# Window-attention block on one core: the gated product re-sorted by DMA, the projection in four quadrants, attention stages and channel units regrouped

## What is computed

```python
x_n = group_norm(x, 32 groups)                        # mean and variance of 2 channels over the image
qkv = einsum('bchw,oc->bohw', x_n, w_qkv) + b_qkv     # 1x1, 64 -> 192 channels
qkv = depthwise_conv3x3(qkv, w_dw) + b_dw             # padding 1
# windows of 8x8 pixels, 4 heads of 16 channels; x runs over the 64 pixels of a window
attn = softmax(einsum('nhcx,nhdx->nhcd', q, k) * temperature)
out  = einsum('nhcd,nhdx->nhcx', attn, v)
gate = gelu(einsum('nhcx,yx->nhcy', v, w_mlp) + b_mlp)
out  = out * gate
y    = x + einsum('bchw,oc->bohw', back_to_image(out), w_proj) + b_proj
```

## Time and profile before

| | |
|---|---|
| median of 3 runs | 679.36 us (678.96 to 680.39) |
| profiled execution, its own time | 681.82 us |
| its span, first to last instruction | 680.0 us |
| TensorE busy | 625.8 us (92%) |
| VectorE busy | 511.6 us (75%) |
| ScalarE busy | 482.8 us (71%) |
| mean granted TensorE clock | 0.973 |
| 16 DMA engines, share of the transfers of the SP queue | 31.0% |

### The profile page before, as it was taken

How to read it: one execution, slowest core, us unless ns; L and a number is a source line. 1 busy time by engine, 2 the same in 40 slices (tenths; PEclk the granted TensorE clock), 3 DMA queues, 4 the chain that set the end, 5 groups by cost and what they waited for, 6 DMA issues and landing times.

```text
span 680.0 us, 32438 instructions
## 1 busy us (share of the span) xinstructions
PE 625.8 (92%) x15044; PEld 549.1 (81%) x15044; DVE 511.6 (75%) x790; ACT 482.8 (71%) x631; POOL 0.3 (0%) x5
## 2 busy tenths in 40 slices
PE   3788799999999999999999999999999999999954
PEld 2687698888989898888989898888989798888843
DVE  4872688887888888786878676786868676876684
ACT  3652678787877778786877778786877778786722
POOL 0000000000000000000000000000000000000000
PEclk9997899999999999999999999999999999999975
DMA  9872115335171714132050504132150504112022
GB/s 363 263 217 72 33 50 166 110 86 208 33 232 49 234 59 149 66 102 93 8 191 5 195 4 142 60 94 106 29 173 4 198 3 152 44 50 80 4 82 44
DMA packets 29240, 72.28 MB, mean 106 GB/s; under 512 B 9801, under 2 KB 16329, under 8 KB 24233
## 3 DMA queue, kind: packets, MB, share of 16 engines
q1 hardware_dynamic: 28674, 68.57, 31.0%
q10 hardware_dynamic: 432, 1.65, 0.7%
HBM read 53.44 MB, written 16.78 MB: 103 GB/s over the span
## 4 chain that ended last, share of the span: by engine, by line
PE 87%; ACT 5%; DVE 3%; issue 2%; DMA 1%; ACTq 0%; DVEq 0%
PE unit_ps L709 28%; PE unit_ps L674 26%; PE rest_ps L796 10%; PE rest_ps L787 6%; PE rest_ps L763 6%; PE rest_ps L747 6%; PE rest_ps L773 4%; ACT z L326 2%; DMA patches<-in_hot 1%; ACT dw L326 1%; PE rest_ps L643 1%; PE rest_ps L674 1%; PE unit_ps L636 0%; DVE scores L511 0%; DVE scores L536 0%
## 5 line engine op out<-in xcount | busy, mean ns | idle before, releaser
L326 ACT ACTIVATE z<-unit_ps 100x768 f32<-100x768 f32 x244 | 184.9, 808 | 60.1 <-PE unit_ps L674 60.1
L674 PE MATMUL unit_ps<-consts,patches 64*100 64x192 f32 x1984 | 195.0, 336 | 8.6 <-ACT z L326 6.6
L709 PE MATMUL unit_ps<-z,dw 103*64 103x64 f32 (+2 forms) x6144 | 194.3, 224 | 3.0 <-issue 1.7
L709 PEld LDWEIGHTS unit_ps<-z,dw 103*64 103x64 f32 (+2 forms) x6144 | 185.5, 139 | 10.7 <-issue 8.6
L674 PEld LDWEIGHTS unit_ps<-consts,patches 64*100 64x100 f32 x1984 | 153.6, 164 | 25.8 <-ACT z L326 11.2
L326 ACT ACTIVATE qkv<-unit_ps 128x1024 f32<-128x1024 f32 x78 | 79.1, 1014 | 31.5 <-PE unit_ps L709 31.4
L511 DVE TENSOR_TENSOR scores<-rest_ps,consts 128x512 f32<-128x512 f32 x64 | 44.1, 689 | 51.6 <-PE rest_ps L747 51.6
L503 DVE TENSOR_TENSOR gate<-rest_ps,gate 128x512 f32<-128x512 f32 x64 | 44.1, 689 | 47.5 <-PE rest_ps L787 44.6
L796 PE MATMUL rest_ps<-gate,consts 128*128 128x256 f32 x256 | 75.1, 417 | 1.1 <-DVE gate L503 1.0
L347 ACT ACTIVATE v_t<-rest_ps 128x512 f32<-128x512 f32 x64 | 38.2, 597 | 40.5 <-PE rest_ps L773 38.9
L341 ACT ACTIVATE scores<-scores 128x512 f32<-128x512 f32 x64 | 40.4, 631 | 33.2 <-DVE scores L518 31.6
(11 more groups left out here) (55 smaller groups left out, 530.5 us busy)
## 6 DMA issues: line engine op xcount, KB each, us to landing
staged<-in_x SPq DMA_DIRECT2D x17, 1024.0 KB, 4.9
out_y<-staged SPq DMA_DIRECT2D x15, 1024.0 KB, 5.4
T<-in_x SPq DMA_DIRECT2D x12, 1152.0 KB, 6.7
seen<-in_x SPq DMA_DIRECT2D x32, 256.0 KB, 2.9
qkv<-in_x SPq DMA_DIRECT2D x6, 1024.0 KB, 13.9
T<-in_x SPq DMA_DIRECT2D x3, 1088.0 KB, 6.7
staged<-in_x SPq DMA_DIRECT2D x2, 512.0 KB, 22.9
out_y<-staged SPq DMA_DIRECT2D x4, 256.0 KB, 3.0
```

The lines of the kernel that those rows point to most:

```text
L326: return nc.scalar.activation(to, of, ACT.Copy)
L674: last = nc.tensor.matmul(to[0:NPATCH, t, b * QKV:(b + 1) * QKV], patches[image, b, g], w1[image], start=True, stop=True)
L709: last = nc.tensor.matmul(to[h * HW:(h + 1) * HW, m // 8, m % 8 * NW:(m % 8 + 1) * NW], dw[0:used, c, :], z[0:used, c, :], start=True, sto ...
```

## The change

1. **Projection.** Before, the gated product lay as VectorE wrote it (each 64-partition half holding a mixture of head halves), and two products with 128x128 stationary operands, mostly zeros, sorted and projected it. Now SP copies the gated product of a step with eight SBUF-to-SBUF transfers of 32x256 elements into `by_row` (`to_rows`), and four products with 64x64 stationary operands, one for each quadrant of the array, project it. It runs two steps later instead of one (`project(i - 2)` in step i), and the last step keeps the old form (`project_last`). `gate` has four buffers instead of three.
2. **Turning v.** In a0 and a1 `turn_v` makes eight products of 64 rows of v with a 64x64 identity instead of four transposes. a2 and a3 keep the transposes.
3. **Gates.** The gate products of step i+2 stand in steps a0 and a1, one each, and two in a3; one of those in a3 goes into a unit buffer. The first two stand before step 0, among the first depthwise units, together with their Gelus.
4. **Order.** Within a step TensorE does score, project, gates, turn_v, then all units of the step in one stretch, then apply_probs.

The core of the diff:

```diff
 def gates_in(i):
-    return (0, 1) if i == 0 else (i + 1, i + 2) if i % 2 and i + 2 < STEPS else ()
+    n, a = i // BATCHES + 1, i % BATCHES
+    if a < 2:
+        return (i + 2,)
+    return (i + 1, i + 2) if a == 3 and n < CHUNKS else ()
+
+def in_unit(j):
+    return j > 1 and j % BATCHES == 1
...
+            def to_rows(j):
+                sp.wait_ge(mixed_ready, j + 1)
+                if j > 1:
+                    sp.wait_ge(proj_done, j - 1)
+                for b in range(2):
+                    for h in range(2):
+                        for t in range(2):
+                            here, there = 2 * (h ^ b) + t, 2 * b + h
+                            sp.dma_start(by_row[there * BLOCK:(there + 1) * BLOCK, j % 2, t],
+                                         gate[here * BLOCK:(here + 1) * BLOCK, j % GATES, b].rearrange(
+                                             "p g y -> p (g y)")).then_inc(by_row_in[j % 2], 16)
...
+            for i in range(STEPS):
+                n, a = i // BATCHES, i % BATCHES
+                if i:
+                    to_rows(i - 1)
...
                 if a < 2:
-                    if more:
-                        evacuate_mix(act, copy, n, 8 * a)
-                        evacuate_mix(act, copy, n, 8 * a + 1)
-                    exponent(i)
-                    v_up(i)
-                    if more:
-                        for g in range(8 * a + 2, 8 * a + 6):
+                    if i == 0 or not more:
+                        v_up(i)
...
                     exponent(i)
                     if more:
+                        if i:
+                            for g in range(3):
+                                evacuate_mix(act, copy, n, 8 * a + g)
+                            v_up(i)
+                        for g in range(3 if i else 2, 6):
+                            evacuate_mix(act, copy, n, 8 * a + g)
...
                 n, a = i // BATCHES, i % BATCHES
                 dve.wait_ge(proj_done, i + 1)
+                if i + 2 < STEPS:
+                    dve.wait_ge(v_t_ready, i + 3)
...
             def turn_v(i):
...
+                    if i % BATCHES < 2:
+                        for h in range(2):
+                            rows = slice(h * HW, (h + 1) * HW)
+                            last = nc.tensor.matmul(turn_ps[:, h, g * HW:(g + 1) * HW], v[rows], ident[rows, rows],
+                                                    start=True, stop=True)
...
             def project(i):
 
+                pe.wait_ge(by_row_in[i % 2], 128 * (i // 2 + 1))
+                if i < STEPS - BATCHES:
+                    pe.wait_ge(mixed_ready, i + 2)
+                if i:
+                    pe.wait_ge(out_ready, i)
+                for t in range(2):
+                    for b in range(2):
+                        rows = slice(b * HW, (b + 1) * HW)
+                        last = nc.tensor.matmul(projected(i)[t * C:(t + 1) * C, b, :], proj_row[rows],
+                                                by_row[rows, i % 2, t].rearrange("p (g r c) -> p r g c", r=WS, c=WS),
+                                                start=True, stop=True)
...
-                if i % BATCHES == 0:
-                    qkv_of(i // BATCHES)
                 if i == 0:
-                    fill(units_now[:cut[0]])
-                score(i)
...
+                score(i)
...
+                if i > 1:
+                    project(i - 2)
+                for j in now:
+                    gates(j, i)
                 if i:
+                    turn_v(i)
+                fill(units_now[4:] if i == 0 else units_now)
+                if i == STEPS - 1:
                     project(i - 1)
-                turn_v(i)
-                fill(units_now[cut[0]:cut[1]])
-                if now:
-                    gates(now[1], i)
-                fill(units_now[cut[1]:cut[2]])
                 apply_probs(i)
-                fill(units_now[cut[2]:])
-            project(STEPS - 1)
+            project_last(STEPS - 1)
```

More of the change, by code:

```diff
@@ L66, in units @@
     for i in range(STEPS):
-        order += fillers(i)
+        order += [("gate", j) for j in gates_in(i) if in_unit(j)] + fillers(i)
     return {name: at for at, name in enumerate(order)}
@@ L365, in _ @@
             deviation(0)
-            exp_table(0)
             for g in range(0, COLS, 2):
                 evacuate_first(act, copy, g)
-            for v in range(0, 6, 2):
-                evacuate_dw(act, copy, 0, v)
+            evacuate_dw(act, copy, 0, 0)
+            evacuate_dw(act, copy, 0, 2)
+            gelu(0)
+            gelu(1)
+            exp_table(0)
+            evacuate_dw(act, copy, 0, 4)
             tables = 1
@@ L582, in _ @@
             normalise(1, 1)
-            for v in range(1, 6, 2):
-                evacuate_dw(dve, copy, 0, v)
+            evacuate_dw(dve, copy, 0, 1)
+            gate_up(0)
+            gate_up(1)
+            evacuate_dw(dve, copy, 0, 3)
+            evacuate_dw(dve, copy, 0, 5)
             for i in range(STEPS):
@@ L739, in score @@
                     pe.wait_ge(masked, i)
[L740 removed]
+                pe.wait_ge(gate_biased, max([2] + [beside_scores(j) for m in range(i) for j in gates_in(m)]))
                 for g in range(BATCH):
```

161 lines of the change are left out of this document (98 added, 63 removed).

## The result

The changed kernel takes **769.94 us** (median of four runs, 756.73 to 774.94) against 679.2 us: ratio **1.121** (95% interval 1.108 to 1.134). The ratio leaves out two of the four runs, which ran at a lower granted clock; the two in it took 767.0 and 756.7 us. It is slower, as forecast, but by twice as much as the 722 us of the forecast, and outside 700 to 742.

A forecast was written before the change was run, and what follows sets the result against it. TensorE, 92% busy, bounds the kernel before. +2.9 us a chunk gives +40.6 over fourteen; +2.4 statistics, -1 first chunk, +0.7 tail make +42.7 on 681.8: 724.5, less 2.5, 722 us; range 700 to 738, chance 0.76, or to 742.

The forecast's parts named there:

- the step that sets the sign: 1x1 units in a0 and a1: two buffers need 1.80 us for two units, against 1.30 us of TensorE work.
- The regrouping's saving: 1x1 units in one stretch: a pair needs 1.30 us instead of 1.53, saving some 1.5 us a chunk on TensorE.
- a0 and a1: First two steps of a chunk: 10.57 us each against 9.08 and 9.91, together +2.15 us.
- I keep 0.54: Turning v in a0 and a1: eight products take 0.54 us, with 0.85 as upper bound.
- The -0.10 forecast: Third step of a chunk, a2: 8.29 us, a change of -0.10 us.
- a3: Last step of a chunk: late first depthwise unit delays ScalarE's run, so next score comes at 11.5 against 10.67, +0.83 us.
- The regular part together: All four steps of a steady chunk: 40.94 us against 38.05, +2.9 us.
- The SP transfers stay off the path: Row transfers: eight issue in 2.5 us and land in 2.9, against at least 8.6 us until the projection needs them.
- Rival 4, the clock: Granted clock falls: one spell costs up to 6.9 us, three or more make it 740 us and up; chance 0.06.
- the chunks with statistics: Four chunks gathering the second pair's statistics: one more VectorE instruction ending a2 delays a3's product, +2.4 us in all.
- Head and tail: First chunk: -1 us, from a vanished stall and one pair of table loads; last four steps: +0.7 us.
- +0.5 a step at most: Last four steps, without units: v_up now before the exponent costs at most 0.5 us a step.

The follow-up runs named there:

- experiment 3: Changed kernel with v turned by transposes everywhere and units spread between the attention stages again, copies in old order: 688.85 us, ratio 1.017.
- Experiment 2: Changed kernel with v turned by four transposes in a0 and a1 too, instead of eight products: 752.23 us, ratio 1.110.
- experiment 9: Changed kernel with ScalarE copying only half of each 1x1 unit: 732.99 us, ratio 1.078.
- Experiment 10: Changed kernel with one depthwise unit of a3 directly behind the score again: 754.65 us, ratio 1.111.
- experiment 4: Kernel before, with eight idle row copies a step and the large store and load moved to a2 and a3: 703.0 us, ratio 1.037.
- 7: Changed kernel with transposes everywhere, units spread again, and large transfers early, in a0 and a1: 680.32 us, ratio 1.001.
- experiment 8: Changed kernel with the old projection, no row transfers, and large transfers early, in a0 and a1: 771.81 us, ratio 1.136.
- experiments 4 to 6: Besides experiment 4, kernel before with late large transfers and no copies, 688.23 us (1.014); with idle copies and large transfers at old places, 683.95 us (1.007).
- experiments 1: Changed kernel with the projection as before, two steps late, without row transfers: 771.99 us, ratio 1.139.

## Why the forecast had the sign and missed the size

**What bounds it, and the step that sets the sign: right.** The forecast read 1.80 us for two units through two buffers against 1.30 us of work, hidden by the attention stages between pairs. After the change pairs stand 1.76 to 1.80 us apart, undoing the stretch takes 63 us off (experiment 3 against 2), and a shorter copy shortens the pitch (experiment 9). Waits of the weight loads for these copies come to 4.5 us a chunk (62.4 us in chunks 1 to 14; forecast 5 to 6), ScalarE is idle for 2.60 us before the exponent (2.5), and TensorE's share is 82% (below 85). The regrouping's saving never appears, since waits fill each pair: TensorE's busy time in a1 is 9.70 us. The section "Tiling Modes" of the page "TensorEngine Tiling (Array Packing)" of the Trainium skill, that a change of mode drains TensorE, agrees with 1.53 against 1.30 us a pair before; no run here shows a gain from it.

**a0 and a1: right in kind, short by 0.4 and 0.5 us.** The first unit stands 432.18 - 429.02 = 3.16 us behind the score, not 2.65. Of the 0.51, the turning is 0.41: **the term "I keep 0.54" failed**; eight products in two row halves measured 0.95, above its upper bound of 0.85 too. The other 0.1 is the gates, which start at 1.59 as forecast (1.6) and take 0.62 us instead of 0.5. The projection starts 0.13 us later than forecast and takes 0.55 us (forecast 0.43), but it ends by the time at which the gates can start, so this costs nothing here.

**a2: 8.48 against 8.29.** Here the projection counts: it starts at 1.04 us instead of 0.96 and takes 0.59 us to the transposes instead of 0.43. The -0.10 forecast became +0.09.

**a3: right to 0.1 us; what came on top are breaks.** The forecast put the first depthwise unit at 3.39 us behind the score, its copy at 5.58 and the next score at 11.51. Experiment 2, which has the same a3, has it at 3.36, 5.55 and 11.45 in two chunks where nothing holds it up. In the changed kernel the unit also stands at 538.48 - 535.12 = 3.36 in three chunks, but each time the units behind it are held up at a packet end; here they take 544.63 - 538.48 = 6.15 us instead of 5.75:

```profile
535.12 0.65 PE L801 MATMUL rest_ps<-qkv 64*64 64x64 f32 x32
538.48 6.22 PE L763 MATMUL unit_ps<-z,dw 103*64 103x64 f32 x192
544.63 0.69 PE L859 MATMUL rest_ps<-v_t,probs_t 64*64 64x64 f32 x32
```

In the chunk of the windows above a packet end falls into the second group of gate products, so that the unit stands at 452.38 - 448.56 = 3.82 us and its copy at 6.02. The shortest a3, 11.77, is of two chunks in which VectorE's product with the gate starts 0.32 us later. Experiment 10 shows that the first unit's place sets a3's end.

**The regular part together**: 42.3 us a chunk at best, forecast 40.94, short by 1.34, or 19 us over fourteen chunks. 0.26 of the 1.34 is a3's and so is no error of the forecast's sum.

**"The SP transfers stay off the path": this step failed.** By it the rows were priced only by when they land. They do land in time: the page gives 2.2 us each, and in the middle the projection starts 0.10 us after VectorE's product with the gate or straight behind the score. What the step did not ask is what sixteen more issues for every two steps, and the large transfers moved to a2 and a3 beside them, do to TensorE's supply of instructions, which they delay: 18.7 us lost at packet ends against 2.2 before. Beside the order of before they cost 25 us together (experiment 4), with no computing engine waiting for the copies; the early places give 8.5 us back (7 against 3). The changed kernel itself with its large transfers early was not run. Issues also took twice their forecast 0.31 us. The SP row beside the break shown above, in the changed kernel:

```profile
578.52 6.13 SPq L306 DMA_DIRECT2D by_row<-gate  x8
```

**Rival 4, the clock, was not rare.** It had 0.06; five spells of 3.4 or 6.8 us at 1.2 GHz lie in chunks 1 to 14. Three stand at the start of a0, behind a wait of the score of 1.65 us (one with a break of 0.79 us as well), in steps of 13.99, 14.55 and 12.04 us instead of 10.97, 7.7 us together; the two others go with breaks of 2.0 and 2.1 us in a3, as at 582. The forecast looked for the danger in the small idle times between pairs of units. There the clock held at 1.00 in all rows above; it fell at single waits of 1.6 to 2.1 us, one of which (the score's, of 1.65 us) the forecast's own a3 contained. So that oscillation of a rule in "TensorE: Matmul & The Clock Gate" of the Trainium skill (section "A second HAM failure mode: psum-queue depth-cycling"), named beside the rival, is not seen inside the stretch here. Breaks and clock make most of the irregular 23 us, of which the forecast had 2.4 (the chunks with statistics: in experiment 8 their a3 are 0.6 us longer, as forecast). How the 23 divide between breaks and clock I can't settle: in experiment 8 the breaks are gone and clock spells took 7.8 us, but the median did not move.

**Head and tail.** The start gained 2.8 us (forecast 1), by luck: its spell at 1.2 GHz lasted 3.4 us instead of 13.7, and the fifth step at 106.8 us is no earlier than in experiments 4 to 6 (104.9 to 106.5). The tail lost 5.2, forecast 0.7 (the sum leaves out the forecast's own "+0.5 a step at most"). Of this 1.7 us lie in the last step, where a projection waits for all of its rows, whose eight issues alone take 4.95 us. The other 3.6 lie in the three steps before it, and experiments 1 and 8, without rows, have tails of 42.2 and 42.1 us where the changed kernel has 41.5. So the rows are not what makes the tail long; what in the new order does stays open. TensorE and then SP at the end of the changed kernel:

```profile
756.10 1.13 PE L874 MATMUL unit_ps<-by_row,consts 64*64 64x256 f32 x8 [4.28 <-DMA by_row<-gate]
```

```profile
749.84 4.95 SPq L306 DMA_DIRECT2D by_row<-gate  x8
```

**The miss in one sum**: 85.2 measured less 42.7 forecast is 42.5 us: 19 in the regular chunk, 20.5 in breaks and clock, 4.5 in the tail, less 1.8 at the head (0.3 is rounding and the chunk of before, 38.05 in the forecast and 38.0 here). The range reached to half of rival 4, but added no two of these at once.

## What to carry to other kernels

Where producer and copy share two buffers, compare their cycle (start to copy, copy, signal back) with the producer's work before grouping units together: other stages between pairs are cover, and here they were worth more than the changes of tile shape that they brought. Price transfers on a queue not only by when they land but by what they run beside: keep large ones out of the steps in which TensorE gets through the most instructions (here a2 with 281 records in 8.5 us, against 185 in 11.0 in a0), look for TensorE groups that break off with "issue" as the releaser, and count the records between the breaks. Fewer or smaller products on an engine save nothing until its next wait is gone, and a step forecast with a wait of TensorE like the 1.65 us here should carry a price for the clock too.

## What the runs showed of the hardware

- Eight fp32 products with a 64-row, 128-column stationary operand and 64 moving columns take 0.95 us (16 records), where 16 products with 64x64 stationary operands and the same columns take 0.62 (431.23 - 430.61). The weight loads of the eight, 128 columns wide, fill 0.97 us of it, those of the sixteen 0.56.
- A transfer of 32x256 elements from SBUF to SBUF took SP 0.6 to 0.8 us to issue when eight stood in a row, and landed in 2.2 us.
- Beside idle copies and late large transfers TensorE broke off in the middle of a group for up to 2.23 us (experiment 4). In all 86 breaks of fourteen traces this happened at the same place in its stream of records, modulo 256, and it went on 2.1 to 3.3 us after the start of a packet of its instruction queue.
- Behind identical waits of 1.65 us the clock fell to 1.2 GHz in five chunks of one run (experiment 8) and kept 2.4 GHz in the others.
